# A two-layer perceiver kernel: alignment distances go from their tiles to the lanes by 32 transfers inside SBUF instead of by way of DRAM, and the backtracking flags are made with one more product

## The reference

```
D = sqrt(max(|a|^2 + |b|^2 - 2 a.b, 0))                 # 257 x 32 distances
R[i, j] = D[i, j] + min(R[i-1, j], R[i, j-1], R[i-1, j-1])
from (256, 31) back to (0, 0):
    choice = argmin(R[i-1, j-1], R[i-1, j], R[i, j-1])  # the first of equals
    out[j] += context[i]                                # for each cell (i, j) on the path
x = x + out
```

## Time and profile before

| | us |
|---|---|
| median of 3 runs | 2040.63 |
| lowest, highest | 2037.58, 2048.53 |
| the profiled execution | 2038.24 |
| its span in the trace | 2036.4 |
| PE busy | 1754.5 (86%) |
| DVE busy | 1130.5 (56%) |
| POOL busy | 773.5 (38%) |
| ACT busy | 659.6 (32%) |

### The profile page before, as it was taken

The page is one execution under the profiler, slowest core; times in us unless marked ns, Lnnn a source line. Parts: engine busy times, 40 slices in busy tenths (PEclk is TensorE's granted clock), DMA queues, the critical chain, the costliest instruction groups (busy, mean ns, idle before and its releaser), DMA issues.

```text
span 2036.4 us, 22701 instructions
## 1 busy us (share of the span) xinstructions
PE 1754.5 (86%) x8422; PEld 843.7 (41%) x8422; DVE 1130.5 (56%) x1519; ACT 659.6 (32%) x1175; POOL 773.5 (38%) x427
## 2 busy tenths in 40 slices
PE   7888877978999999999998668999703989789998
PEld 4666654442332332333325343444401457534443
DVE  3444443198999999999993333222367463521111
ACT  2333432233554555555551220111313140111121
POOL 1443332007998998999992110000200023000000
PEclk8999997997999999999997668999755779689999
DMA  2111101011000000001004100010180100101110
GB/s 70 31 31 36 31 16 50 3 55 46 13 9 25 11 10 25 10 10 25 10 5 170 56 0 16 31 46 15 30 178 2 31 0 1 42 0 41 42 41 21
DMA packets 34945, 65.51 MB, mean 32 GB/s; under 512 B 12740, under 2 KB 21848, under 8 KB 33188
## 3 DMA queue, kind: packets, MB, share of 16 engines
q1 hardware_dynamic: 34868, 64.49, 10.7%
HBM read 55.80 MB, written 8.67 MB: 32 GB/s over the span
## 4 chain that ended last, share of the span: by engine, by line
PE 51%; POOL 19%; DVE 14%; issue 11%; DMA 2%; ACT 2%; SPq 0%; DVEq 0%; ACTq 0%; POOLq 0%
POOL arena L1006 18%; PE ps L1222 6%; PE ps L1972 5%; PE ps L1984 5%; PE ps L198 4%; PE ps L1235 3%; PE ps L339 3%; PE ps L344 3%; PE ps L221 2%; DVE arena L934 2%; PE ps L357 2%; DVE arena L474 2%; PE ps L1747 2%; PE ps L1763 1%; PE ps L214 1%
## 5 line engine op out<-in xcount | busy, mean ns | idle before, releaser
L1006 POOL TENSOR_TENSOR arena<-arena 128x1024 f32<-128x1024 f32 x248 | 577.9, 2377 | 23.9 <-DVE arena L960 17.8
L787 PE MATMUL ps<-arena 32*128 32x512 f32 x2016 | 471.8, 640 | 24.4 <-DVE arena L941 19.3
L892 ACT ACTIVATE arena<-arena 128x1024 f32<-128x1024 f32 x248 | 262.2, 1057 | 294.1 <-DVE arena L950 294.1
L963 DVE TENSOR_TENSOR arena<-arena,ps 128x1024 f32<-128x1024 f32 x248 | 302.5, 1220 | 9.9 <-POOL arena L1006 8.7
L950 DVE TENSOR_TENSOR arena<-arena,ps 128x1024 f32<-128x1024 f32 x248 | 301.2, 1215 | 8.0 <-PE ps L787 8.0
L787 PEld LDWEIGHTS ps<-arena 32*128 32x128 f32 x2016 | 163.2, 187 | 334.5 <-issue 144.9
L2042 DVE TENSOR_TENSOR arena<-arena,ps 128x512 f32<-128x512 f32 x64 | 44.0, 688 | 183.5 <-ACT arena L2017 171.4
L811 PE MATMUL ps<-arena 128*32 128x512 f32 x1024 | 139.6, 618 | 5.2 <-DVE arena L963 3.1
L1222 PE MATMUL ps<-arena 128*128 128x512 f32 x288 | 131.1, 600 | 5.9 <-DVE arena L1093 5.9
L1929 POOL TENSOR_TENSOR arena<-arena 128x1024 f32<-128x1024 f32 x16 | 30.0, 1896 | 240.0 <-DVE arena L1862 225.3
L1972 PE MATMUL ps<-arena 128*128 128x512 f32 x256 | 116.8, 600 | 0.0
(11 more groups left out here) (263 smaller groups left out, 2249.0 us busy)
## 6 DMA issues: line engine op xcount, KB each, us to landing
arena<-ctxT SPq DMA_DIRECT2D x32, 257.0 KB, 3.1
arena<-ctxT SPq DMA_DIRECT2D x8, 1028.0 KB, 14.4
arena<-L_ffn_w SPq DMA_DIRECT2D x16, 512.0 KB, 4.2
arena<-ctx_rows SPq DMA_DIRECT2D x8, 960.0 KB
m_rows<-arena SPq DMA_DIRECT2D x16, 256.0 KB, 2.5
arena<-m_rows SPq DMA_DIRECT2D x64, 64.0 KB
arena<-L_ffn_eW SPq DMA_DIRECT2D x8, 512.0 KB, 3.6
m_yd<-arena SPq DMA_DIRECT2D x64, 32.0 KB
```

The lines of the kernel that those rows point to most:

```text
L787: mm = nc.tensor.matmul(ps[:, ring(n) + jj, :], weights[r], m_row[r, buf, t % CH, :], start=True, stop=True)
L892: nc.scalar.activation(m_xa[:, u, t % 2], m_xa[:, u, t % 2], ACT.Exp, scale=-1.0).then_inc(S["m_dec"], 1)
L963: nc.vector.tensor_tensor(m_h[:, u, t % 2], m_xa[:, u, t % 2], ps[:, ring(n):ring(n) + 2, :], ALU.add).then_inc(S["m_use"], 1)
L1006: nc.gpsimd.tensor_tensor(m_xa[:, u, t % 2], m_xa[:, u, t % 2], m_h[:, u, (t - 1) % 2], ALU.mult).then_inc(S["m_kept"], 1)
```

## The change

The DRAM tensor is not used any more. For each batch one DMA takes the 32 partitions of its tile (1044 bytes each) and writes them one behind the other into one partition, lane b of the first group, so that `d_D` holds all three segments there (34 slots x 3 x 87). When all 32 have landed, DVE copies segment 2 to lane group 2 and half of segment 1 to lane group 1, and ACT the other half. The new `d_D` lies where the context of tiles 0 to 4 was, hence SP's new wait for `d_ab` 5 ahead of the first transfer. The places of the context rows `d_ct` change; the last two lie over `d_D` and are loaded only when the forward pass has ended (`d_fwd`).

Of the five flag operations three stay in form: the third now makes `stay` (1 where the path does not go up). Then `dg` = `dg` x `stay`, `lf` = `stay` - `dg`, and ACT makes `up` = 1 - `stay`.

```
@@ -1403,10 +1403,11 @@
         d_E, d_VD = view(5093, WW), view(5093 + WW, 2, WW)
         d_F = bview(5376, 3, 2 + SLOTS * WW)
         d_V = bview(9816, SLOTS, WW)
+        d_stay = bview(11296, SLOTS, WW)
         d_least = view(12776, SLOTS, WW)
-        d_D = view(EXTRA + 2056, SLOTS, WW)
+        d_D = view(28 * K, SLOTS, SEG * WW)
         d_M = view(12776, SLOTS, PB)
-        d_ct = [view(18696 + 3072 * g, SL, SEG, D) for g in range(TT)]
+        d_ct = [view(o, SL, SEG, D) for o in (*(16 * K + 3072 * g for g in range(4)), 37 * K, EXTRA, 28 * K, 31 * K)]
         ACT_SQ = 5
         TINY = 1e-30
         PER = 3
@@ -1420,23 +1421,17 @@
             return slice(B * k, B * k + B)
 
         def d_load(sp):
-            def keep(g):
+            sp.wait_ge(*S.at("d_ab", 5))
+            for g in range(TT):
                 sp.wait_ge(*S.at("d_sqrt", 2 * g + 2))
-                sp.dma_start(dist[:, g * P:(g + 1) * P].rearrange("k p i -> p k i"), d_dt[g]).then_inc(S[f"d_out{g % 2}"], 16)
-
-            def back(g):
-                sp.wait_ge(*S.at(f"d_out{g % 2}", 16 * (g // 2) + 16))
-                for k in range(SEG):
-                    r = slice(B * k + SL * g, B * k + SL * g + SL)
-                    sp.dma_start(d_D[r, k:k + L].rearrange("p j i -> p (j i)"),
-                                 dist[k, g * P:(g + 1) * P].rearrange("(b j) i -> b (j i)", j=L)).then_inc(S["d_back"], 16)
-            keep(0)
-            for g in range(1, TT):
-                keep(g)
-                back(g - 1)
-            back(TT - 1)
-            sp.wait_ge(*S.at("d_ab", TT))
+                for bi in range(SL):
+                    b = SL * g + bi
+                    sp.dma_start(d_D[b:b + 1, 0:L], d_dt[g][L * bi:L * bi + L].rearrange("p k i -> p (k i)"))\
+                        .then_inc(S["d_back"], 16)
+            sp.wait_ge(*S.at("d_back", 16 * B))
             for g in range(TT):
+                if g == TT - 2:
+                    sp.wait_ge(*S.at("d_fwd", 3 * SLOTS))
                 for r in (slice(0, 80), slice(80, W)):
                     sp.dma_start(d_ct[g][r], A["ctx_rows"][r, g * SL:g * SL + SL]).then_inc(S[f"d_rows{g // 4}"], 16)
 
@@ -1547,9 +1542,15 @@
             squares(4)
             for g in range(1, TT):
                 root(g)
+            act.wait_ge(*S.at("d_back", 16 * B))
+            nc.scalar.copy(d_D[lane(1), 1:1 + L // 2, 0:WW], d_D[lane(0), 0:L // 2, WW:2 * WW]).then_inc(S["d_out0"], 1)
             for s in range(SLOTS):
                 act.wait_ge(*S.at("d_fwd", max(3 * s, 1)))
                 nc.scalar.copy(d_least[lane(1), s, 0:1], d_R[lane(0), s, W:WW]).then_inc(S["d_least"], 1)
+
+            act.wait_ge(*S.at("d_sort", 1))
+            nc.scalar.activation(by_slot(2)[:, :, 1:WW], d_stay[0:PB, :, 1:WW], ACT.Copy, bias=1.0,
+                                 scale=-1.0).then_inc(S["d_out1"], 1)
 
             def turned(first, n):
                 lo, (e, _) = SLOTS - first - n, turned_to(first)
@@ -1597,16 +1598,16 @@
                                         ps[:, g % 4, W - 1:SK].rearrange("p (k i) -> p k i", i=W), own, 0.0, ALU.add,
                                         ALU.max).then_inc(S["d_clip"], 1)
 
-            R, least, D_ = d_R[0:PB], d_least[0:PB], d_D[0:PB]
+            R, least, D_ = d_R[0:PB], d_least[0:PB], d_D[0:PB, :, 0:WW]
             E_, VD, V_ = d_E[0:PB], d_VD[0:PB], d_V[0:PB]
             lf, dg, up = (by_slot(n) for n in range(3))
             ch.step(nc.vector.memset(R[:, 0, :], BIG))
             ch.step(nc.vector.memset(d_least[lane(0), :, 0:1], BIG))
             for k in range(SEG):
                 if k:
-                    ch.step(nc.vector.memset(d_D[lane(k), 0:k], BIG))
+                    ch.step(nc.vector.memset(d_D[lane(k), 0:k, 0:WW], BIG))
                 if k < SEG - 1:
-                    ch.step(nc.vector.memset(d_D[lane(k), k + L:SLOTS], BIG))
+                    ch.step(nc.vector.memset(d_D[lane(k), k + L:SLOTS, 0:WW], BIG))
             ch.step(nc.vector.memset(d_F[0:PB, :, 0:2], 0.0))
             for v in (lf, dg, up):
                 ch.step(nc.vector.memset(v[:, :, 0:1], 0.0))
@@ -1614,7 +1615,10 @@
             ch.sync()
             ch.step(nc.vector.memset(d_E[lane(SEG - 1), 1:2], 1.0))
             ch.link(nc.vector.memset(d_R[lane(0), 0, 1:2], 0.0))
-            dve.wait_ge(*S.at("d_back", 16 * SEG * TT))
+            dve.wait_ge(*S.at("d_back", 16 * B))
+            ch.step(nc.vector.tensor_copy(d_D[lane(2), 2:2 + L, 0:WW], d_D[lane(0), 0:L, 2 * WW:3 * WW]))
+            ch.link(nc.vector.tensor_copy(d_D[lane(1), 1 + L // 2:1 + L, 0:WW], d_D[lane(0), L // 2:L, WW:2 * WW]))
+            dve.wait_ge(*S.at("d_out0", 1))
 
             for s in range(SLOTS):
                 prev = R[:, s]
@@ -1626,15 +1630,15 @@
                                              ALU.min, ALU.add).then_inc(S["d_fwd"], 1)
                 dve.wait_ge(*S.at("d_fwd", 3 * s + 3))
 
-            own = slice(1, WW)
+            own, stay = slice(1, WW), d_stay[0:PB]
             ch.step(nc.vector.tensor_tensor(dg[:, :, W:0:-1], R[:, 0:SLOTS, 0:W], R[:, 0:SLOTS, own], ALU.is_le))
             ch.link(nc.vector.tensor_tensor(least[:, :, own], R[:, 1:SLOTS + 1, 0:W], least[:, :, own], ALU.subtract))
-            ch.link(nc.vector.scalar_tensor_tensor(out=up[:, :, own], in0=dg[:, :, own], scalar=-TINY,
-                                                   in1=least[:, :, W:0:-1], op0=ALU.mult, op1=ALU.is_ge))
-            ch.step(nc.vector.scalar_tensor_tensor(out=lf[:, :, own], in0=dg[:, :, own], scalar=0.0,
-                                                   in1=up[:, :, own], op0=ALU.is_equal, op1=ALU.is_gt))
-            ch.sync()
-            ch.link(nc.vector.tensor_tensor(dg[:, :, own], dg[:, :, own], up[:, :, own], ALU.is_gt))
+            nc.vector.scalar_tensor_tensor(out=stay[:, :, own], in0=dg[:, :, own], scalar=-TINY,
+                                           in1=least[:, :, W:0:-1], op0=ALU.mult, op1=ALU.is_lt).then_inc(S["d_sort"], 1)
+            dve.wait_ge(*S.at("d_sort", 1))
+            ch.link(nc.vector.tensor_tensor(dg[:, :, own], dg[:, :, own], stay[:, :, own], ALU.mult))
+            ch.link(nc.vector.tensor_tensor(lf[:, :, own], stay[:, :, own], dg[:, :, own], ALU.subtract))
+            dve.wait_ge(*S.at("d_out1", 1))
             for k in range(SEG - 1):
                 for v in (1, 2):
                     ch.step(nc.vector.tensor_copy(by_lane(v, k)[:, 0:SLOTS - 1, 0:1], by_lane(v, k + 1)[:, 1:SLOTS, W:WW]))
```

## The result

The changed kernel is slower: 2057.45 us median of 15 runs (2050.45 to 2073.1) against 2041.7 of the kernel before in the same runs (2035.61 to 2053.82); ratio 1.0072, 95% interval 1.0052 to 1.0092. That is 14.7 us of 2041.7. Applied to the 2040.63 given before, the ratio makes 2055.3, near the range's upper end of 2057; the measured median lies 0.45 above that end. Rival A had 2052.5, or 2054.9 counted from the median. The likeliest case, 2041.5, was 14 to 16 us too low.

A forecast was written before the change was run, and what follows sets the result against it. The alignment stage was taken to bound: an 18.2 us hole of DMA carrying, then DVE's chain. Carrying +3.8 and flags -1.5 gave +2.3 us on 2038.24, 2040.5; put at 2041.5, range 2031 to 2057.

The forecast's parts named there:

- Rival A: Drain of the carrying: one small partition group takes only 29.6 GB/s, so 36.1 us and 2052.5 in all; chance 0.30.
- The likeliest case: Whole kernel: carrying +3.8 and flags -1.5 make +2.3 us, put at 2041.5, own range 2034 to 2048; chance 0.50.
- What bounds: Alignment stage: 18.2 us hole before the forward pass, then a DVE chain that moves the end one for one.
- Start: Carrying: SP waits for the fifth tile's product and starts at 1465.4, when DVE's clip of that tile starts.
- Fixed latency: Carrying: a small load lands after 1.7 us.
- Drain: Carrying: 1069 KB into single partitions at 44.4 GB/s take 24.1 us, distances there at 1491.2.
- Issue: SP's queue: 32 issues take 10.7 us at 0.293 us each, up to 18.5 us at 0.537 us each.
- Case B: Carrying: only SP's issue limits, forward pass at 1480.4 to 1488.2, time 2027.1 to 2034.9; chance 0.15.
- the sign that I had set for A: SP's queue: 32 issues stretching out beyond 20 us mean the queue is backed up and A (Rival A) holds.
- Lane copies: Before the forward pass: DVE's two copies to lanes 1 and 2 add 2.5 us, ACT's 1.4 hidden behind them.
- Flags: Between forward and backward steps: two products of 1.7 us replace two operations, ACT's 2.6 us beside them: -1.5 us.
- Moved loads: Context rows issued after the last distance landed: no cost, 36 us of cover before PE's expansion wants the first.

The follow-up runs named there:

- e3: Changed kernel with only the first of three segments carried, a third of the bytes: SP's first transfer to first lane copy 22.1 us, against 37.4.
- e5: Changed kernel, same 32 transfers after all roots, one of each tile in turn: first transfer to first lane copy 22.6 us, against 37.4.
- e4: Changed kernel with each tile's four batches in lanes eight apart: first lane copy after 23.2 us; ratio to the kernel before 0.9991.
- e1: Changed kernel with every second of a tile's transfers sent to the partition 64 further on: first transfer to first lane copy 23.0 us, against 37.4.
- e6: Kernel before, by way of DRAM, with lanes eight apart: forward pass 28.3 us after the first clip instead of 33.0; ratio 0.9995.
- e8: Changed kernel with lanes eight apart, half the transfers issued by ACT: first lane copy after 22.0 us; ratio to the kernel before 1.0027.
- e9: e8 with only the first segment carried, a third of the bytes: first lane copy 14.1 us after SP's first transfer.
- e10: e8 with ACT's half of the transfers sent to the partition 64 further on: first lane copy after 21.1 us, 0.9 less than e8.

## Why the prediction was right and wrong

The range holds the measured time only because rival A had set its upper end; the sum itself was 14 to 16 us too low, and the forward pass started 49.8 us after the first clip, just outside the 23 to 49 beyond which I had called myself wrong (1480 to 1506, with the first clip at 1457.0).

*What bounds.* Right: the hole ahead of the forward pass and the chain behind it are on the path one for one; +15.1 us there gave 14.7 in the time.

*Start.* 1.4 us late: SP's first transfer comes 9.8 us after the first clip instead of the 8.4 of the earlier trace rows, since the fifth tile's product did so in this execution. The mechanism held.

*Fixed latency.* 1.7 us was used; e3's lane copy, behind its small transfers, started 1.5 us after the last issue ended (1492.01 to 1493.55), which fits.

*Drain: the step that failed.* I wrote "I take 44.4 GB/s, the nearest shape" and "I let these two cancel". They don't. 1506.7 - 1469.35 - 1.7 = 35.6 us for 1069 KB, 30.0 GB/s; rival A had 36.1 us at 29.6 GB/s. The 44.4 GB/s were two groups' rate, one of them carrying two thirds; with all of a tile in one group only that one's 29.6 was left. (Both are a little low: the 130.5 KB of the rows are of 1024 bytes, three loads of four runs of 11,136 bytes are 134 KB of 1000, and both kernels carry 1069 KB. In one unit it is 45.5 and 30.3 GB/s, a drain of 23.5 us in my sum and 35.3 in A's.) That the new transfers can use sixteen engines was worth nothing: with all of them busy, one group of four partitions still took 30 GB/s. My argument against A, that engines run ahead into the next tile's group, is answered by e5: the same transfers with groups alternating in the queue had no jam, four in a row for one group had. How far ahead the engines can run was not measured. The mis-sized term explains 11.5 of the 13.0 us by which the forward pass was later than my sum (49.8 against 1493.8 - 1457.0 = 36.8), the start the other 1.4.

*Issue.* My bound from above, 0.577 us per transfer, was too low: 0.59 and a gap, 20.7 us for 32. Case B could never have come: e4 has no jam and is where the issue puts it, 1.2 us later than before. For the same reason the sign that I had set for A, issues that take over 20 us together, was worthless: they took 20.7 us with the jam, 20.8 in e4 and 20.6 in e1 and e3 without it. What told A was the landing.

*Lane copies.* 1.61 + 0.89 forecast, 1.60 + 0.88 measured; ACT's copy was hidden.

*Flags.* -1.5 forecast, -1.5 measured: from the first wide operation to the first backward step 13.8 us instead of 15.3, with two products of 1.70, ACT's 2.64 beside them and no table load. The 34 forward steps took 28.2 us instead of 28.4, which was not forecast.

*Moved loads.* Right: the context rows were issued from 1506.7 on, the last behind the forward pass, and the expansion's products still began 35.0 us after the first backward step, in both kernels.

*Chances.* 0.55 on no measurable change was too much. Two of three loads into one group, 89 KB per 2.94 us, already gave the group's rate; I had worked it out and gave it 0.30. That the figure came out so exact is in part luck: e6 shows that SP's chain alone would have kept the loads 2.8 us apart.

## What to carry to other kernels

Before moving data by DMA into few partitions, count the bytes per group {p to p + 3, p + 32 to p + 35} along the order of the queue: here one such group took 30 GB/s, though all sixteen DMA engines were busy. Spread neighbours in the queue over groups first, by naming lanes or ordering transfers; then count the issues, for 32 small transfers cost SP 20.7 us, more than the hole that they were to close. A way that looks longer (through DRAM, with 32 larger loads and stores on two queues) was the faster one here.

## What the runs showed of the hardware that I had not expected

- The issue of a transfer costs the queue by its form, not by its bytes: 0.293 us into four neighbouring partitions, 0.556 into four that are eight apart, 0.59 from 32 partitions into one, and that for 33 KB and 11 KB alike (e3, e6). On ACT's queue the same transfer took mostly 0.51 to 0.62 us (e8, e9).
- With two queues and four groups the DMA engines were full at some 60 GB/s, 52 over the whole carrying (e8), and sending half to the other side of partition 64 shortened it by 4% (e10). In a single queue with alternating groups 51 to 53 GB/s were the issue's own pace (e1, e4, e5). So a second issuing queue had little left to win.
